# Gates of the grouped experts on GpSimd, and their last product in three passes on split values

## The chip, the cores and the metric

One core of one Trainium2 chip runs the whole program. The metric is the device time of one execution in microseconds (us), the median of the runs shown. TensorE is PE in the profile, VectorE is DVE, ScalarE is ACT, GpSimd is POOL and SyncE, which issues the DMAs here, is SP; PEld is PE's load of stationary weights.

## The reference, cut to what matters

The program is a tower of four layers on 64 x 32 = 2048 tokens of 128 channels: a choice of tokens, then four times an attention-like and an expert stage. The change lies in the first expert stage alone. It has 64 experts of 64 hidden channels; a router gives each token 8 of them with weights:

```
h  = silu(x @ w1[e]) * (x @ w3[e])
yb = h @ w2[e]
y  = sum over the 8 chosen e of  w[e] * yb
```

An expert takes at most 256 tokens. The kernel computes every expert for every token and multiplies by a gate that is zero where the token is not the expert's, so the expert stage does the same work for any routing.

## The kernel before, in words

The stage `grouped_experts` (line 721) works on 32 units of two experts: the hidden channels of both fill the 128 partitions. A unit has four steps, one for each group of 512 tokens, so there are 128 steps. The channels lie on the partitions and the tokens along the free axis.

A step goes like this. PE makes `pa` = x times w1 and `pb` = x times w3 in PSUM. Each is a `product` (line 303) of three passes in the format fp32r: the high part of the weights times the high part of x, the low part of the weights times the high part of x, and the high part of the weights times the low part of x. ACT makes the silu `S` of `pa` (line 815). DVE multiplies it by `pb` into `T2` ("bend", line 829), and by the gates `GS` into `HF` ("gate", line 838). PE multiplies `HF` by w2 and adds into one of four accumulators `acc` that stay in PSUM over all units (line 794): one product of plain fp32, which the trace records as two.

PE's order is written out by hand: step s of `pa` and `pb`, then the last product of step s - 2. `pa` and `pb` have two PSUM buffers each; a step waits until "bend" of the step before the last has read them (`t_ready`).

Weights come from `Weights` (line 311): SP loads a unit's 128 x 384 numbers (w1, w3, w2) into one of four buffers `W`, and POOL splits the first 256 columns into the high part (line 332, an addition of zero that rounds) and the low part (line 336, a subtraction). The first four units are split in the routing stage (`route_grouped`), where `start_splits` does it; the others are split by POOL as soon as their load has landed, and POOL does nothing else in the stage.

The gates: routing leaves a row of gates for each expert in DRAM; SP loads the two rows of a unit, each broadcast to 64 partitions (line 766), into one of three buffers `GS`. SP's queue is in program order: it waits for the buffer of unit u - 3, loads the gates of unit u, waits until the last products of unit u - 1 are done (`summed`), and loads the weights of unit u + 3.

Other stages do similar things. `quick_experts` (stage m3x) has its gates on POOL (line 634) with the weight splits between them, and its last product in fp32. `relu_experts` (stage m1x) splits its hidden values on chip: high part by ACT (line 500) or DVE, low part by DVE (line 532), then a product of three passes.

Of the kernel before, what the change touches and what calls it, by code (L numbers as in the profile page):

```python
# [13 lines left out]
F32 = mybir.dt.float32  # L14
BF16 = mybir.dt.bfloat16
F32R = mybir.dt.float32r
U32 = mybir.dt.uint32
ALU = mybir.AluOpType
ACT = mybir.ActivationFunctionType
AX = mybir.AxisListType  # L20

P = 128
# [4 lines left out]
GROUP = 512  # L27
GROUPS = T // GROUP
# [274 lines left out]
def product(pe, out, lhsT, rhs, start=True, stop=True):  # L303


    pe.matmul(out, lhsT[0], rhs[0], start=start, stop=False, skip_group_check=True)  # L306
    pe.matmul(out, lhsT[1], rhs[0], start=False, stop=False, skip_group_check=True)  # L307
    return pe.matmul(out, lhsT[0], rhs[1], start=False, stop=stop, skip_group_check=True)  # L308
# [43 lines left out]
class ReluWeights:  # L352


    RAW = 4
# [212 lines left out]
def quick_experts(nc, name, H, XR, ident, gateF, gate_rows, stored, weights, b2):  # L568


    UNITS = 16
    STEPS = UNITS * GROUPS
    RAW = weights.buffers
    W, WR, BX = weights.W, weights.WR, weights.BX
    w_loaded, w_split, bias_ready = weights.loaded, weights.split_made, weights.bias_ready
    with Stage(nc, name) as st:
# [28 lines left out]
        with nc.Block() as block:  # L605
            @block.sync
            def _(sp):
                sp.dma_start(B2[:, :], b2[:, :]).then_inc(bias_loaded, 16)
                sp.wait_ge(stored, 16 * GROUPS)
                for u in range(UNITS):  # L610
                    e = u // 2
                    if u % 2 == 0:
                        if e >= 2:
                            sp.wait_ge(gated, 2 * GROUPS * (e - 1))
                        sp.dma_start(GS[:, e % 2, :], gate_rows[e, :].partition_broadcast(P)).then_inc(g_loaded[e % 2], 16)
                    if u >= 1 and u + RAW - 1 < UNITS:
                        sp.wait_ge(summed, GROUPS * u)
# [103 lines left out]
def grouped_experts(nc, name, H, XR, ident, gate_rows, stored, weights):  # L721

    UNITS = 32
    STEPS = UNITS * GROUPS
    RAW = weights.buffers
    GB = 3  # L730
    W, WR = weights.W, weights.WR
    w_loaded, w_split = weights.loaded, weights.split_made
    with Stage(nc, name) as st:
        GS = st.sb("GS", [P, GB, T])
        S = st.sb("S", [P, 2, GROUP])
        T2 = st.sb("T2", [P, 2, GROUP])
        HF = st.sb("HF", [P, 3, GROUP])
        OT = st.sb("OT", [P, T])
        acc = [st.ps(f"acc{g}", [P, GROUP]) for g in range(GROUPS)]
        pa = [st.ps(f"pa{i}", [P, GROUP]) for i in range(2)]  # L740
        pb = [st.ps(f"pb{i}", [P, GROUP]) for i in range(2)]
        g_loaded = [st.sem(f"g_loaded{i}") for i in range(GB)]
        a_ready = st.sem("a_ready")
        b_ready = st.sem("b_ready")
        s_ready = st.sem("s_ready")
        t_ready = st.sem("t_ready")
        gated = st.sem("gated")
        summed = st.sem("summed")
        ot_ready = st.sem("ot_ready")
        turned = st.sem("turned")  # L750

        def place(s):
            return s // GROUPS, s % GROUPS

        def tokens(g):
            return slice(g * GROUP, (g + 1) * GROUP)

        with nc.Block() as block:
            @block.sync
            def _(sp):  # L760
                sp.wait_ge(stored, 16 * GROUPS)
                for u in range(UNITS):
                    if u >= GB:
                        sp.wait_ge(gated, GROUPS * (u - GB + 1))
                    for e in range(2):
                        sp.dma_start(GS[64 * e:64 * (e + 1), u % GB, :],
                                     gate_rows[2 * u + e, :].partition_broadcast(64)).then_inc(g_loaded[u % GB], 16)
                    if u >= 1 and u + RAW - 1 < UNITS:
                        sp.wait_ge(summed, GROUPS * u)
                        weights.load(sp, u + RAW - 1, (u + RAW - 1) % RAW)  # L770

            @block.gpsimd
            def _(pool):
                for u in range(RAW, UNITS):
                    pool.wait_ge(w_loaded[u % RAW], 16 * (u // RAW + 1))
                    weights.split(nc.gpsimd, u % RAW, u, None)

            @block.tensor
            def _(pe):
                def first(s):  # L780
                    u, g = place(s)
                    j = u % RAW
                    if g == 0:
                        pe.wait_ge(w_split, RAW + u + 1)
                    if s >= 2:
                        pe.wait_ge(t_ready, s - 1)
                    x = [XR[:, n, tokens(g)] for n in range(2)]
                    product(pe, pa[s % 2][:, :], [WR[:, j, n, 0:P] for n in range(2)], x).then_inc(a_ready, 1)
                    product(pe, pb[s % 2][:, :], [WR[:, j, n, P:2 * P] for n in range(2)], x).then_inc(b_ready, 1)

                def second(s):
                    u, g = place(s)
                    pe.wait_ge(gated, s + 1)
                    pe.matmul(acc[g][:, :], W[:, u % RAW, 2 * P:3 * P], HF[:, s % 3, :], start=(u == 0),  # L794
                              stop=(u == UNITS - 1), skip_group_check=True).then_inc(summed, 1)

                for s in range(STEPS + 2):
                    if s < STEPS:
                        first(s)
                    if s >= 2:  # L800
                        second(s - 2)
                for g in range(GROUPS):
                    pe.wait_ge(ot_ready, g + 1)
                    out = (pa[0], pa[1], pb[0], pb[1])[g]
                    for t in range(GT):
                        mm = pe.transpose(out[:, t * P:(t + 1) * P], OT[:, (g * GT + t) * P:(g * GT + t + 1) * P], ident[:, :])
                    mm.then_inc(turned, 1)

            @block.scalar
            def _(act):  # L810
                for s in range(STEPS):
                    act.wait_ge(a_ready, s + 1)
                    if s >= 2:
                        act.wait_ge(t_ready, s - 1)
                    nc.scalar.activation(S[:, s % 2, :], pa[s % 2][:, :], ACT.Silu).then_inc(s_ready, 1)  # L815
                for g in range(GROUPS):
                    act.wait_ge(summed, STEPS - GROUPS + g + 1)
                    nc.scalar.activation(OT[:, tokens(g)], acc[g][:, :], ACT.Copy).then_inc(ot_ready, 1)

            @block.vector  # L820
            def _(dve):
                v = nc.vector

                def bend(s):
                    dve.wait_ge(s_ready, s + 1)
                    dve.wait_ge(b_ready, s + 1)
                    if s >= 2:
                        dve.wait_ge(gated, s - 1)
                    v.tensor_tensor(T2[:, s % 2, :], S[:, s % 2, :], pb[s % 2][:, :], ALU.mult).then_inc(t_ready, 1)  # L829

                def gate(s):
                    u, g = place(s)
                    dve.wait_ge(t_ready, s + 1)
                    if g == 0:
                        dve.wait_ge(g_loaded[u % GB], 32 * (u // GB + 1))
                    if s >= 3:
                        dve.wait_ge(summed, s - 2)
                    v.tensor_tensor(HF[:, s % 3, :], T2[:, s % 2, :], GS[:, u % GB, tokens(g)], ALU.mult).then_inc(gated, 1)  # L838

                for s in range(STEPS + 1):  # L840
                    if s < STEPS:
                        bend(s)
                    if s:
                        gate(s - 1)
                for g in range(GROUPS):
                    t = slice(g * GT, (g + 1) * GT)
                    dve.wait_ge(turned, g + 1)
                    out = (pa[0], pa[1], pb[0], pb[1])[g]
                    v.tensor_tensor(H[:, t, :], H[:, t, :], out[:, :].rearrange("p (t c) -> p t c", c=P), ALU.add)
# [1961 lines left out]
def build(nc, ins, out):  # L2811
    Stage.spent = []
    with Stage(nc, "g") as st:
# [32 lines left out]
        with Stage(nc, "m0s") as s:  # L2846
            XR = s.sb("XR", [P, 2, T], F32R)
            GT_rows = s.sb("GT_rows", [64, T])
            gate_rows = nc.dram_tensor("m0_gate_rows", (64, T), F32, kind="Internal").ap()
            stored = s.sem("stored")  # L2850
            weights = Weights(nc, s, ins["L0_units"], 4, 2 * P, 0)
            route_grouped(nc, "m0r", XT, XR, ident, iota, consts["earlier"], ins["L0_ffn_gate_w"], ins["L0_ffn_gate_b"],
                          GT_rows, gate_rows, stored, weights)
            grouped_experts(nc, "m0x", H, XR, ident, gate_rows, stored, weights)
# [18 lines left out]
        with Stage(nc, "m3s") as s:  # L2873
# [4 lines left out]
            weights = Weights(nc, s, ins["L3_units"], 4, 2 * P, 3)  # L2878
# [108 lines left out]
```

## Time and profile before

| | us |
|---|---|
| runs of the kernel | 3297.12, 3297.83, 3304.19 (median 3297.83) |
| the profiled execution | 3300.3, with a span of 3298.5 from its first to its last instruction |
| the stage of the grouped experts in that span | 1295.0 to about 1592 |
| mean granted clock of PE over the span | 0.888 of full speed |

The profile is of one execution. A line of a timeline gives the start in us from the start of the span, the duration in us, the engine, the line of the kernel, the operation, what it writes and reads with partitions x elements, how many records are merged, and in brackets the idle time before it and what ended it. Names carry the stage: `m0x_` is the stage of the change, `m0s_` its weights.

### The profile page before, as it was taken

Reading aid. Unit: us, or ns where it says so; the run is one execution under the profiler, and the core shown is the slowest. Engines: PE = TensorE matmul, PEld = TensorE weight load, DVE = VectorE, ACT = ScalarE, POOL = GpSimd, SP = SyncE. Lnnn points to the kernel's source line nnn. Section 1 sums busy time; section 2 is a strip of 40 time slices with the busy share of each in tenths; the row PEclk is TensorE's granted clock in tenths of the full one; section 3 lists DMA queues with packets and bytes.
Section 4 is the critical chain, followed back from the end, with each engine's and each line's share of the span. In section 5 each row is a group of like instructions: output and inputs, shape, how many; then the busy total and the mean of one; then the engine's idle time right before and its main releaser. Section 6 shows DMA issues by size and latency. Waiting matters only on the chain. (4 is left out here: it accounts for less than half of the span.)

```text
span 3298.5 us, 29241 instructions
## 1 busy us (share of the span) xinstructions
PE 2573.4 (78%) x8955; PEld 1522.9 (46%) x8955; DVE 2360.9 (72%) x3401; ACT 1333.6 (40%) x2106; POOL 1386.7 (42%) x841
## 2 busy tenths in 40 slices
PE   1887877687787754999578978399997589768499
PEld 0333333332332322666346646377775467523365
DVE  5699798669979975555566575578886668669556
ACT  2644544264454421222243433167774257410222
POOL 1499699449969951111114334100001210024266
PEclk9899899889989886999789989599998789879799
DMA  4244155125505502556100000121210021000021
GB/s 135 41 122 109 20 130 108 29 41 122 109 20 129 109 21 56 138 137 150 33 17 10 16 0 4 36 76 60 76 57 13 3 89 52 17 13 13 11 81 64
DMA packets 86601, 203.32 MB, mean 62 GB/s; under 512 B 12816, under 2 KB 25184, under 8 KB 77920
## 3 DMA queue, kind: packets, MB, share of 16 engines
q1 hardware_dynamic: 85952, 200.63, 24.0%
q8 instruction: 63, 1.03, 0.1%
q0 software_dynamic: 512, 1.05, 0.1%
q14 instruction: 74, 0.61, 0.1%
HBM read 198.76 MB, written 2.88 MB: 61 GB/s over the span
## 5 line engine op out<-in xcount | busy, mean ns | idle before, releaser
L532 DVE TENSOR_TENSOR m1x_HS<-m1x_R,m1x_HS 128x512 fp32r<-128x512 f32 x256 | 175.8, 691 | 69.2 <-ACT m1x_HS L500 64.8
L493 ACT ACTIVATE m1x_R<-m1x_ph,m1s_W 128x512 f32<-128x512 f32 x256 | 176.3, 689 | 107.1 <-PE m1x_ph L308 106.3
L1337 POOL TENSOR_TENSOR t2x_KM<-t2x_KT,t2x_HM 128x2048 f32<-128x2048 f32 x8 | 28.8, 3603 | 434.8 <-ACT t2x_KT L1410 416.6
L1677 POOL TENSOR_TENSOR t3xs_QH<-t3xs_HS,t3xa_Q 128x1536 f32<-128x1536 f32 x16 | 62.0, 3877 | 352.6 <-DVE t3xs_HS L1663 352.6
L829 DVE TENSOR_TENSOR m0x_T<-m0x_S,m0x_pb 128x512 f32<-128x512 f32 x128 | 88.1, 689 | 128.3 <-PE m0x_pb L308 120.8
L2080 PE MATMUL t0x1fs_acc<-t0x1fs_HC,g_ident 128*128 128x512 f32 x256 | 134.1, 656 | 38.2 <-POOL t0x1fs_HC L2161 38.1
L2080 PE MATMUL t0x0fs_acc<-t0x0fs_HC,g_ident 128*128 128x512 f32 x256 | 135.0, 660 | 36.4 <-POOL t0x0fs_HC L2161 36.3
L815 ACT ACTIVATE m0x_S<-m0x_pa 128x512 f32<-128x512 f32 x128 | 76.6, 598 | 213.1 <-PE m0x_pa L308 213.1
L2080 PE MATMUL t0x1bs_acc<-t0x1bs_HC,g_ident 128*128 128x512 f32 x256 | 130.8, 641 | 37.1 <-POOL t0x1bs_HC L2161 37.0
L2080 PE MATMUL t0x0bs_acc<-t0x0bs_HC,g_ident 128*128 128x512 f32 x256 | 130.4, 640 | 35.8 <-POOL t0x0bs_HC L2161 35.7
L2161 POOL TENSOR_TENSOR t0x1bs_HC<-t0x1bs_HS,t0x1bs_CB 128x1024 f32<-128x1024 f32 x64 | 149.2, 2360 | 13.2 <-PE t0x1bs_acc L2080 6.6
L2161 POOL TENSOR_TENSOR t0x0bs_HC<-t0x0bs_HS,t0x0bs_CB 128x1024 f32<-128x1024 f32 x64 | 149.3, 2370 | 9.8 <-DMA t0x0bs_CB<-t0x0b_bc_rows 3.6
L2161 POOL TENSOR_TENSOR t0x1fs_HC<-t0x1fs_HS,t0x1fs_CB 128x1024 f32<-128x1024 f32 x64 | 149.1, 2370 | 6.0 <-DMA t0x1fs_CB<-t0x1f_bc_rows 4.5
L2161 POOL TENSOR_TENSOR t0x0fs_HC<-t0x0fs_HS,t0x0fs_CB 128x1024 f32<-128x1024 f32 x64 | 148.7, 2354 | 5.6 <-DMA t0x0fs_CB<-t0x0f_bc_rows 3.9
L332 POOL TENSOR_TENSOR m0s_WR<-m0s_W,m0s_ZERO 128x256 fp32r<-128x256 f32 x32 | 26.2, 820 | 260.7 <-DMA m0s_W<-in_L_units 260.5
L794 PE MATMUL m0x_acc<-m0x_HF,m0s_W 128*128 128x512 f32 x256 | 131.6, 596 | 5.3 <-DVE m0x_HF L838 5.3
L532 DVE TENSOR_TENSOR m2x_HS<-m2x_R,m2x_HS 128x512 fp32r<-128x512 f32 x128 | 87.9, 692 | 43.1 <-ACT m2x_HS L500 40.9
L493 ACT ACTIVATE m2x_R<-m2x_ph,m2s_W 128x512 f32<-128x512 f32 x128 | 88.2, 689 | 53.7 <-PE m2x_ph L308 53.3
L634 POOL TENSOR_TENSOR m3x_HF<-m3x_T,m3x_GS 128x512 f32<-128x512 f32 x64 | 81.6, 1280 | 59.1 <-DVE m3x_T L706 57.2
L306 PE MATMUL m1x_py<-m1x_HS,m1s_WR 128*128 128x512 f32 x256 | 103.3, 404 | 1.4 <-DVE m1x_HS L532 1.3
L306 PE MATMUL m0x_pa<-m0s_XR,m0s_WR 128*128 128x512 f32 x128 | 100.9, 788 | 1.8 <-PEq L890 1.8
L307 PE MATMUL m1x_ph<-m1s_XR,m1s_WR 128*128 128x512 f32 x256 | 102.3, 400 | 0.0
(908 smaller groups left out, 7652.2 us busy)
## 6 DMA issues: line engine op xcount, KB each, us to landing
m0x_GS<-m_gate_rows SPq DMA_DIRECT2D x64, 512.0 KB, 6.6
t0x0fs_CB<-t0x0f_bc_rows SPq DMA_DIRECT2D x32, 512.0 KB, 6.1
t0x0bs_CB<-t0x0b_bc_rows SPq DMA_DIRECT2D x32, 512.0 KB, 6.4
t0x1fs_CB<-t0x1f_bc_rows SPq DMA_DIRECT2D x32, 512.0 KB, 6.3
t0x1bs_CB<-t0x1b_bc_rows SPq DMA_DIRECT2D x32, 512.0 KB, 6.8
m1x_GS<-m_gate_rows SPq DMA_DIRECT2D x16, 1024.0 KB, 4.7
m1s_W<-in_L_w SPq DMA_DIRECT2D x16, 514.0 KB, 3.3
m2x_GS<-m_gate_rows SPq DMA_DIRECT2D x8, 1024.0 KB, 4.7
```

Of the source, the lines that this page charges most:

```text
L306: pe.matmul(out, lhsT[0], rhs[0], start=start, stop=False, skip_group_check=True)
L307: pe.matmul(out, lhsT[1], rhs[0], start=False, stop=False, skip_group_check=True)
L493: a.activation(R[:, s % 4, :], ph[s % 4][:, :], ACT.Relu, bias=W[:, e % RAW, weights.cut + c:weights.cut + c + 1]).then_inc(relu_ready, 1)
L532: v.tensor_tensor(HS[:, s % 4, 1, :], R[:, s % 4, :], HS[:, s % 4, 0, :].bitcast(F32), ALU.subtract).then_inc(low_made, 1)
L634: nc.gpsimd.tensor_tensor(HF[:, s % 3, :], T2[:, s % 2, :], GS[:, u // 2 % 2, tokens(g)], ALU.mult).then_inc(gated, 1)
L794: pe.matmul(acc[g][:, :], W[:, u % RAW, 2 * P:3 * P], HF[:, s % 3, :], start=(u == 0), stop=(u == UNITS - 1), skip_group_check=True).then_ ...
L815: nc.scalar.activation(S[:, s % 2, :], pa[s % 2][:, :], ACT.Silu).then_inc(s_ready, 1)
L829: v.tensor_tensor(T2[:, s % 2, :], S[:, s % 2, :], pb[s % 2][:, :], ALU.mult).then_inc(t_ready, 1)
L1337: nc.gpsimd.tensor_tensor(KM[:, i % 2, :, :], keys, spread(HM[:, :], W), ALU.mult).then_inc(km_made, 1)
L1677: nc.gpsimd.tensor_tensor(QH[:, j % 2, 0:SPLIT], HS[:, j % 2, 0:SPLIT], Q[:, 0:SPLIT], ALU.mult).then_inc(qh_pool, 1)
L2080: mm = pe.matmul(acc[:, dh, :], ident[:, :], HC[:, m % 3, dh, :], start=False, stop=False, skip_group_check=True)
L2161: nc.gpsimd.tensor_tensor(HC[:, m % 3, :, :], HS[:, m % 5, :, :], rows, ALU.mult).then_inc(hc_made, 1)
```

## The change

The gates move from DVE to POOL and to an earlier place: POOL multiplies the silu `S` by the gates into `SG`, and "bend" multiplies `SG` by `pb` into `HF`. ACT then copies `HF`, rounded, into the high half of `HR`, and DVE subtracts to get the low half ("low"). The last product takes three passes on the two halves of `HR` and of w2, so the weights are split in all 384 columns. It follows three steps behind instead of two (`LAG`). POOL's queue now holds the gates of every step, and the weight split of unit u + 1 behind the gates of step 1 of unit u. ACT's queue holds the silu of step s and then the copy of step s - 2. SP loads the gates of two units ahead, and of three units at the start. `first` waits for the silu ahead of `pa`, and for "bend" ahead of `pb`.

```diff
-    W, WR = weights.W, weights.WR
+    WR = weights.WR
+    LAG = 3
...
-        T2 = st.sb("T2", [P, 2, GROUP])
-        HF = st.sb("HF", [P, 3, GROUP])
+        SG = st.sb("SG", [P, 2, GROUP])
+        HF = st.sb("HF", [P, 2, GROUP])
+        HR = st.sb("HR", [P, 4, 2, GROUP], F32R)
...
-                for u in range(UNITS):
-                    if u >= GB:
-                        sp.wait_ge(gated, GROUPS * (u - GB + 1))
+
+                def load_gates(u):
                     for e in range(2):
                         sp.dma_start(GS[64 * e:64 * (e + 1), u % GB, :],
                                      gate_rows[2 * u + e, :].partition_broadcast(64)).then_inc(g_loaded[u % GB], 16)
+
+                for u in range(GB - 1):
+                    load_gates(u)
+                for u in range(UNITS):
+                    if u + GB - 1 < UNITS:
+                        if u:
+                            sp.wait_ge(gated, GROUPS * u)
+                        load_gates(u + GB - 1)
                     if u >= 1 and u + RAW - 1 < UNITS:
                         sp.wait_ge(summed, GROUPS * u)
                         weights.load(sp, u + RAW - 1, (u + RAW - 1) % RAW)
...
-                for u in range(RAW, UNITS):
-                    pool.wait_ge(w_loaded[u % RAW], 16 * (u // RAW + 1))
-                    weights.split(nc.gpsimd, u % RAW, u, None)
+                for s in range(STEPS):
+                    u, g = place(s)
+                    if g == 0:
+                        pool.wait_ge(g_loaded[u % GB], 32 * (u // GB + 1))
+                    pool.wait_ge(s_ready, s + 1)
+                    if s >= 2:
+                        pool.wait_ge(hidden, s - 1)
+                    nc.gpsimd.tensor_tensor(SG[:, s % 2, :], S[:, s % 2, :], GS[:, u % GB, tokens(g)], ALU.mult).then_inc(gated, 1)
+                    if g == 1 and RAW <= u + 1 < UNITS:
+                        pool.wait_ge(w_loaded[(u + 1) % RAW], 16 * ((u + 1) // RAW + 1))
+                        weights.split(nc.gpsimd, (u + 1) % RAW, u + 1, None)
...
                     if s >= 2:
-                        pe.wait_ge(t_ready, s - 1)
+                        pe.wait_ge(s_ready, s - 1)
                     x = [XR[:, n, tokens(g)] for n in range(2)]
                     product(pe, pa[s % 2][:, :], [WR[:, j, n, 0:P] for n in range(2)], x).then_inc(a_ready, 1)
+                    if s >= 2:
+                        pe.wait_ge(hidden, s - 1)
                     product(pe, pb[s % 2][:, :], [WR[:, j, n, P:2 * P] for n in range(2)], x).then_inc(b_ready, 1)

                 def second(s):
                     u, g = place(s)
-                    pe.wait_ge(gated, s + 1)
-                    pe.matmul(acc[g][:, :], W[:, u % RAW, 2 * P:3 * P], HF[:, s % 3, :], start=(u == 0),
-                              stop=(u == UNITS - 1), skip_group_check=True).then_inc(summed, 1)
-
-                for s in range(STEPS + 2):
+                    pe.wait_ge(low_ready, s + 1)
+                    product(pe, acc[g][:, :], [WR[:, u % RAW, n, 2 * P:3 * P] for n in range(2)],
+                            [HR[:, s % 4, n, :] for n in range(2)], u == 0, u == UNITS - 1).then_inc(summed, 1)
+
+                for s in range(STEPS + LAG):
                     if s < STEPS:
                         first(s)
-                    if s >= 2:
-                        second(s - 2)
+                    if s >= LAG:
+                        second(s - LAG)
...
-                for s in range(STEPS):
-                    act.wait_ge(a_ready, s + 1)
+                for s in range(STEPS + 2):
+                    if s < STEPS:
+                        act.wait_ge(a_ready, s + 1)
+                        if s >= 2:
+                            act.wait_ge(gated, s - 1)
+                        nc.scalar.activation(S[:, s % 2, :], pa[s % 2][:, :], ACT.Silu).then_inc(s_ready, 1)
                     if s >= 2:
-                        act.wait_ge(t_ready, s - 1)
-                    nc.scalar.activation(S[:, s % 2, :], pa[s % 2][:, :], ACT.Silu).then_inc(s_ready, 1)
+                        n = s - 2
+                        act.wait_ge(hidden, n + 1)
+                        if n >= 4:
+                            act.wait_ge(summed, n - 3)
+                        nc.scalar.activation(HR[:, n % 4, 0, :], HF[:, n % 2, :], ACT.Copy).then_inc(high_ready, 1)
...
                 def bend(s):
-                    dve.wait_ge(s_ready, s + 1)
+                    dve.wait_ge(gated, s + 1)
                     dve.wait_ge(b_ready, s + 1)
                     if s >= 2:
-                        dve.wait_ge(gated, s - 1)
-                    v.tensor_tensor(T2[:, s % 2, :], S[:, s % 2, :], pb[s % 2][:, :], ALU.mult).then_inc(t_ready, 1)
-
-                def gate(s):
-                    u, g = place(s)
-                    dve.wait_ge(t_ready, s + 1)
-                    if g == 0:
-                        dve.wait_ge(g_loaded[u % GB], 32 * (u // GB + 1))
-                    if s >= 3:
-                        dve.wait_ge(summed, s - 2)
-                    v.tensor_tensor(HF[:, s % 3, :], T2[:, s % 2, :], GS[:, u % GB, tokens(g)], ALU.mult).then_inc(gated, 1)
+                        dve.wait_ge(low_ready, s - 1)
+                    v.tensor_tensor(HF[:, s % 2, :], SG[:, s % 2, :], pb[s % 2][:, :], ALU.mult).then_inc(hidden, 1)
+
+                def low(s):
+                    dve.wait_ge(high_ready, s + 1)
+                    v.tensor_tensor(HR[:, s % 4, 1, :], HF[:, s % 2, :], HR[:, s % 4, 0, :].bitcast(F32),
+                                    ALU.subtract).then_inc(low_ready, 1)

                 for s in range(STEPS + 1):
                     if s < STEPS:
                         bend(s)
                     if s:
-                        gate(s - 1)
+                        low(s - 1)
...
-            weights = Weights(nc, s, ins["L0_units"], 4, 2 * P, 0)
+            weights = Weights(nc, s, ins["L0_units"], 4, 3 * P, 0)
```

## Rows read from the trace of the kernel before

**Rows 1.** The page, part 1: busy time, share and instructions of each engine.
```profile
PE 2573.4 (78%) x8955; PEld 1522.9 (46%) x8955; DVE 2360.9 (72%) x3401; ACT 1333.6 (40%) x2106; POOL 1386.7 (42%) x841
```

**Rows 2.** Windows: stretch, length, busy us of each engine, clock, DMA, GB/s.
```profile
1304.00:1310.00 6.00, 5.92 (x16) 3.78 (x17) 2.61 (x5) 0.91 (x2) 0.00 (x0) 0.73 0.45 94
...
1370.00:1390.00 20.00, 20.00 (x73) 13.39 (x72) 11.45 (x19) 5.38 (x9) 4.44 (x6) 1.00 0.64 152
...
3000.00:3040.00 40.00, 34.04 (x78) 14.15 (x77) 37.48 (x30) 0.00 (x0) 19.37 (x5) 1.00 0.06 16
```

**Rows 3.** Timeline of one step in the middle of the stage, PE and ACT.
```profile
1400.98 0.39 PE L307 MATMUL m0x_pa<-m0s_XR,m0s_WR 128*128 128x512 f32 x1
...
1401.21 0.40 PE L308 MATMUL m0x_pa<-m0s_XR,m0s_WR 128*128 128x512 f32 x1
...
1401.64 0.60 ACT L815 ACTIVATE m0x_S<-m0x_pa 128x512 f32<-128x512 f32 x1 [1.64 <-PE m0x_pa L308]
...
1403.22 0.39 PE L307 MATMUL m0x_pa<-m0s_XR,m0s_WR 128*128 128x512 f32 x1
```

**Rows 4.** Groups of instructions by line: busy us, mean ns, idle before.
```profile
L634 POOL TENSOR_TENSOR m3x_HF<-m3x_T,m3x_GS 128x512 f32<-128x512 f32 x64 | 81.6, 1280 | 59.1 <-DVE m3x_T L706 57.2 <-PE m3x_acc L657 1.1 <-issue 0.8
...
L336 POOL TENSOR_TENSOR m0s_WR<-m0s_W,m0s_WR 128x256 fp32r<-128x256 f32 x32 | 23.2, 726 | 2.5
...
L500 ACT ACTIVATE m1x_HS<-m1x_R 128x512 fp32r<-128x512 f32 x128 | 79.7, 623 | 0.0
...
L532 DVE TENSOR_TENSOR m1x_HS<-m1x_R,m1x_HS 128x512 fp32r<-128x512 f32 x256 | 175.8, 691 | 69.2 <-ACT m1x_HS L500 64.8
```

**Rows 5.** Timeline, DVE and POOL where they overlap, in two stages.
```profile
1214.69 4.50 POOL L1059 TENSOR_TENSOR g_H<-g_H,t0x1o_GB 128x2048 f32<-128x2048 f32 x1 [11.22 <-SPq L1027]
...
1217.96 1.27 DVE L91 TENSOR_TENSOR t0x1l_mean<-t0x1l_stats 128x16 f32<-128x16 f32 x1
1219.15 0.17 DVE L92 TENSOR_TENSOR t0x1l_gap<-t0x1l_stats 128x16 f32<-128x16 f32 x1
...
1315.52 0.68 DVE L838 TENSOR_TENSOR m0x_HF<-m0x_T,m0x_GS 128x512 f32<-128x512 f32 x1
1315.91 0.90 POOL L332 TENSOR_TENSOR m0s_WR<-m0s_W,m0s_ZERO 128x256 fp32r<-128x256 f32 x1 [62.71 <-DMA m0s_W<-in_L_units]
1316.89 0.72 POOL L336 TENSOR_TENSOR m0s_WR<-m0s_W,m0s_WR 128x256 fp32r<-128x256 f32 x1
1317.17 0.69 DVE L829 TENSOR_TENSOR m0x_T<-m0x_S,m0x_pb 128x512 f32<-128x512 f32 x1 [0.96 <-PE m0x_pb L308]
```

**Rows 6.** Timeline, gates on POOL in the stage m3x.
```profile
3149.65 0.75 DVE L706 SCALAR_TENSOR_TENSOR m3x_T<-m3x_pb,m3s_BX,m3x_T 128x512 f32<-128x512 f32 x1
...
3150.48 1.27 POOL L634 TENSOR_TENSOR m3x_HF<-m3x_T,m3x_GS 128x512 f32<-128x512 f32 x1 [0.53 <-DVE m3x_T L706]
...
3171.78 2.53 POOL L634 TENSOR_TENSOR m3x_HF<-m3x_T,m3x_GS 128x512 f32<-128x512 f32 x2
```

**Rows 7.** Timeline, the last early weight split, and the start and end of the stage.
```profile
1252.48 0.72 POOL L336 TENSOR_TENSOR m0s_WR<-m0s_W,m0s_WR 128x256 fp32r<-128x256 f32 x1
...
1303.34 0.69 DVE L838 TENSOR_TENSOR m0x_HF<-m0x_T,m0x_GS 128x512 f32<-128x512 f32 x1 [4.54 <-DMA m0x_GS<-m_gate_rows]
...
1304.09 2.07 PE L794 MATMUL m0x_acc<-m0x_HF,m0s_W 128*128 128x512 f32 x2 [4.69 <-DVE m0x_HF L838]
...
1306.81 0.60 PE L308 MATMUL m0x_pa<-m0s_XR,m0s_WR 128*128 128x512 f32 x1
1307.23 0.40 PE L306 MATMUL m0x_pb<-m0s_XR,m0s_WR 128*128 128x512 f32 x1
...
1309.03 0.40 PE L307 MATMUL m0x_pa<-m0s_XR,m0s_WR 128*128 128x512 f32 x1
...
1584.66 0.39 PE L307 MATMUL m0x_pa<-m0s_XR,m0s_WR 128*128 128x512 f32 x1
...
1589.44 0.60 ACT L818 ACTIVATE m0x_OT<-m0x_acc 128x512 f32<-128x512 f32 x1 [0.26 <-PE m0x_acc L794]
```

More of the change, by code:

```diff
@@ L745, in grouped_experts @@
         s_ready = st.sem("s_ready")
-        t_ready = st.sem("t_ready")
         gated = st.sem("gated")
+        hidden = st.sem("hidden")
+        high_ready = st.sem("high_ready")
+        low_ready = st.sem("low_ready")
         summed = st.sem("summed")
```

## The prediction

> **What bounds the kernel now.** The page's busy shares [rows 1] mix all stages and decide nothing here; only the stage of the grouped experts (1295 to 1592 us) changes. The windows [rows 2] show TensorE (PE) busy 20.00 of 20 us there at a granted clock of 1.00, the level of 2.4 GHz, with VectorE (DVE) at 11.45, ScalarE (ACT) at 5.38, GpSimd (POOL) at 4.44. So PE's own work is the bound. The timeline gives its step: from one second pass of the pa product (1400.98) to the next (1403.22) are 2.24 us [rows 3]. A split pass takes 0.23 us (1400.98 to 1401.21). Six make 1.38, so the plain fp32 product of line 794 takes 2.24 - 1.38 = 0.86. The stage is 32 units of 4 steps.
>
> **What the change takes off PE.** The fp32 product becomes three split passes, 3 x 0.23 = 0.69, and a step of nine passes 2.07 us: 0.17 us less, 21 us in 124 steps. The same three-pass product on values split on chip runs in stage m1x behind ACT's copy and DVE's subtraction [rows 4]. That is the gain, if PE stays the bound.
>
> **What it puts elsewhere.** Per step: the gates go from DVE (0.68, line 838 [rows 5]) to POOL, where the same 128x512 product takes 1.28 [rows 4], or 1.25 when it queues behind another (two in 2.53 [rows 6]); ACT gains a rounding copy, 0.62; DVE gains the subtraction ("low"), 0.69 [rows 4]. Per unit POOL also makes the weight split, now 384 columns wide, right behind the gates of step 1. No row has 384 columns; between 256 (0.73, line 336) and 512 (1.28) the middle is 1.00 each, ends 0.73 and 1.28. POOL's sum per unit is 4 x 1.28 + 2 x 1.00 = 7.1 of 8.28 us: by itself it fits. DVE, 1.38 of 2.07, and ACT, 1.22, fit too.
>
> **What doesn't fit: POOL and DVE don't read at once.** Rows 5 show it both ways. DVE's line 838 (both inputs in SBUF) ends at 1316.20; POOL's line 332, begun at 1315.91, ends 0.61 later and is 0.90 long. Line 336, begun later, beside no such instruction, takes 0.72. The other way round: line 91 of DVE, a 0.18 us instruction (line 92 takes 0.17), begins inside POOL's line 1059 and lasts 1.27, to 0.04 after POOL's end. So whichever comes second stands until the first is done, and then needs its duration less about 0.12 (0.72 - 0.61) of lead. Before, this meets one split half per unit, on an engine with 15 us to spare. "Low" reads HF and HR, both in SBUF; POOL's gates and splits read SBUF. "bend" reads PSUM for one input, as line 829 does, which at 1317.17 overlaps line 336 with no loss to either (0.69 and 0.72): I let it run free.
>
> Now one step, counted from its first PE pass. pa is done at 0.86 (its third pass starts at 0.46 and lasts 0.40); ACT's silu runs 0.89 to 1.49 [rows 3]; POOL starts 0.08 after its releaser ends (3150.40 to 3150.48 [rows 6]), the other hand-offs take 0.03 (silu after pa) to 0.08, which no term turns on: gates 1.57 to 2.85. ACT makes the copy for step s-2 right behind the silu, 1.51 to 2.13, so "low" of s-2 is always released inside the gates: it stands from 2.17 to 2.85 and ends 0.55 (0.69 less 0.14) later, at 3.40. "bend" of s follows, 3.44 to 4.13. The last product of s-2, queued behind pb of step s+1, is due at 2.07 + 1.38 = 3.45 and gets its data at 3.46. So a step without a weight split keeps 2.07 with nothing to spare.
>
> Step 1 of a unit, with the split, same zero. Gates end at 2.85; "low" takes its turn to 3.40; first half 3.40 + 0.88 = 4.28; "low" of step 0, behind bend, reads first again, to 4.93; second half 4.93 + 0.88 = 5.81. (Were the half first: 5.36, "low" to 5.91, gates of step 2 at 7.05: no difference.) Only now the gates of step 2, due at 3.64: to 7.06. bend 7.14 to 7.83. Queued behind it on PE is pb of the next unit's step 0, which needs bend's PSUM buffer: due 6.90, starts 7.88, ends 8.57. The gates of step 3 run to 8.31 and hold up "low" of step 1 to 8.86, so its last product, due at 8.57, runs 8.92 to 9.61. There the next unit's step 1 starts, with POOL idle and the same state as at the zero. A unit with a split takes 9.61 us, where the kernel before takes 4 x 2.24 = 8.96.
>
> PE's gaps, 0.98 and 0.35 us per unit, I cost without a fall of the clock: in the recurrence stage PE is busy 34.04 of 40 us at clock 1.00 [rows 2].
>
> How ready instructions take turns is not in the rows. My order (the one that stood first reads first) costs 1.33 us a unit over 8.28. Below: if no turn were lost, readings of 4 x 1.14 (gates behind a low), 4 x 0.55 and 2 x 1.00 make 8.76. Above: if a turn saves nothing of the second one's lead, the same walk gives 3.54 for "low", 4.54 and 6.23 for the halves ("low" between them to 5.23), 7.48 and 8.73 for the gates, 9.42 for "low" and 10.17 for the unit; a step without a split is then 2.22. I take 9.61, since line 332's row shows the lead saved (0.61 after the turn, not 0.72), and keep both ends.
>
> The Trainium skill, "SBUF — State Buffer", section "Who interferes with whom", has GpSimd and a VectorE instruction with two SBUF inputs exclude each other for the whole instruction, where rows 5 let about 0.12 overlap. By that letter every turn costs the full duration: an estimate of 10.17 a unit and some 3334 in all, against 3316.6 by rows 5.
>
> **Start, end, queues.** The first gates wait for their rows until 1303.34 [rows 7], as before: SP issues six loads instead of four, the first two at the head. Then 1.28 on POOL and 0.69 on DVE: pb of step 2 starts at 1305.45 (last product before: 1304.09). PE ran at the lower of its two levels for some 3.1 us after that wait (1304.09 to 1307.23 [rows 7]; mean clock of the window 0.73 [rows 2]). With as much again, seven passes of 0.42 (1306.81 to 1307.23), then five of 0.23 (rest of pb of step 3, first last product), step 4 starts at some 1309.7 to 1309.8; before it was 1308.8 (1309.03 less a pass): +1.0. At the end step 127 goes through gates, bend, copy, low and three passes: the last copy starts 6.45 after its first pass, against 1589.44 - 1584.43 = 5.01: +1.4. The first four weight splits, longer by 8 x 0.27 us on POOL, lie in the routing stage: the last ends at 1253.2 [rows 7], and nothing reads them before the stage starts at 1295: nothing, and 40 us of cover. Gates now load two units ahead; SP waits for the gates of u-1, some eight steps (16 us) before use: nothing either way.
>
> **Sum.** Steps 4 to 127 are 123. Before: 123 x 2.24 = 275.5. After: 28 units with a split, 28 x 9.61 = 269.1, and 11 steps of 2.07, 22.8: 291.9, so +16.4. With +1.0 and +1.4: +18.8 us on the span of 3298.5. The profiled execution took 3300.3; it would be 3319.1. The median of the runs shown, 3297.83, stands 2.5 below that execution, so I forecast 3316.6.
>
> **The rivals.**
> 1. PE stays the bound (faster). If "low" and POOL read side by side, low of step 1 is never held by gates and only the split's burst counts: gates of step 2 end at 1.57 + 1.28 + 2.08 + 1.25 = 6.18, bend 6.95, pb of the next step 0 waits from 6.90 to 7.0, some 0.1. A unit is then 8.4: 28 x 8.4 + 22.8 = 258.0, -17.5; with +1.0 and +1.0 (a shorter tail) -15.5: 3282. For it: lines 838 and 829 lose nothing before. Against: rows 5.
> 2. The turns pack (no change). At 8.76 per unit: 245.3 + 22.8 = 268.1, -7.4 + 2.4 = -5: 3293; at 9.0 to 9.1, +2 to +5. For it: two steps of a unit have POOL time over. Against: each later instruction is released by the one that stands, so idle turns occur.
> 3. Every turn costs more (slower still): 28 x 10.17 + 11 x 2.22 = 309.2, +33.7 + 2.4: 3334. For it: line 91 shows no lead saved, and POOL might win each tie and keep reading. Against: line 332.
>
> It decides at 8.96 us per unit: reading turns that add under 0.68 to 8.28 leave a gain.
>
> **How the numbers follow.** About 0.2% (6.6 us) is what a measurement can tell from no change. Chances: forecast 0.60, rival 3 0.07, both slower: 0.67; rival 2 0.13, same; rival 1 0.20, faster. The forecast's own range is 3306 to 3327. The range for 8 in 10 takes in rival 2, the nearer part of rival 1 (some 0.07 of its 0.20) and most of rival 3: 3284 to 3331.
>
> **What would show it.** Right: gates on POOL at 1.25 to 1.45 us each, "low" at 1.1 to 1.4 rather than 0.69 in most steps; a unit at 9.6 us; PE idle in the steady stage some 37 us in all, before pb's first pass with bend as releaser and before the last product with low as releaser. The three passes stand 0.23 apart. Wrong: "low" at 0.69 throughout and PE busy 20 of 20 us (rival 1), or a unit near 9.0 with few PE gaps (rival 2). PE's clock below 1.00 in the steady stage would break the sum on another side.

## The result and the profile after

The changed kernel takes 3311.55 us (median) against 3295.09 for the one before, measured on the same chip; the ratio is 1.0059, 95% interval [1.0044, 1.0073]: slower by 14 to 24 us. The forecast was 3316.6 and slower, +18.8 us.

The profiled execution after took 3308.08 us with a span of 3306.2, only 7.7 more than the span before. The stages that the change doesn't touch took some 11.5 us less in that execution, and executions of the kernel before alone spread over 22 us. So all readings below are made inside the stage: its **length** is counted from the first pass of pa to the start of the last copy of the accumulators (ACT's m0x_OT), its **unit** from the first pass of pa to that four steps later.

Before: 1295.01 to 1589.44 [rows 7], 294.4 us. After: 1291.69 to 1605.37, 313.7. That is **+19.3**, where the sum had +18.8.

The page of after, part 1, against [rows 1]:
```profile
PE 2562.3 (77%) x9083; PEld 1540.9 (47%) x9083; DVE 2413.2 (73%) x3401; ACT 1400.3 (42%) x2234; POOL 1598.6 (48%) x969
```
POOL gains 212 us for 128 more instructions, DVE 52 us for as many as before. The window in the middle of the stage, columns as in [rows 2]:
```profile
1370.00:1390.00 20.00, 18.66 (x77) 13.76 (x76) 13.31 (x16) 9.60 (x18) 17.30 (x14) 1.00 0.57 133
```
PE is no longer busy throughout (18.66 of 20), the clock is still 1.00, and POOL is at 17.30 where it was at 4.44. The groups by tile (ns min/median/max, first and last start) say what became long:
```profile
L793 POOL TENSOR_TENSOR m0x_SG<-m0x_S,m0x_GS x128: 1261/1290/1748, 1300.3 to 1600.3; 128x512 f32<-128x512 f32 x128
L858 DVE TENSOR_TENSOR m0x_HF<-m0x_SG,m0x_pb x128: 686/689/691, 1301.6 to 1602.2; 128x512 f32<-128x512 f32 x128
...
L862 DVE TENSOR_TENSOR m0x_HR<-m0x_HF,m0x_HR x128: 686/1137/1426, 1303.4 to 1603.6; 128x512 fp32r<-128x512 f32 x128
```
The bend (line 858, one input in PSUM) has one length; low (line 862, two inputs in SBUF) has any length from 0.69 to 1.43. One unit in the timeline after, matmuls reduced to first passes:
```profile
1402.65 0.39 PE L306 MATMUL m0x_pa<-m0s_XR,m0s_WR 128*128 128x512 f32 x1
...
1404.21 1.29 POOL L793 TENSOR_TENSOR m0x_SG<-m0x_S,m0x_GS 128x512 f32<-128x512 f32 x1 [1.26 <-ACT m0x_S L838]
1404.68 1.36 DVE L862 TENSOR_TENSOR m0x_HR<-m0x_HF,m0x_HR 128x512 fp32r<-128x512 f32 x1 [0.37 <-ACT m0x_HR L844]
1404.69 0.39 PE L306 MATMUL m0x_pa<-m0s_XR,m0s_WR 128*128 128x512 f32 x1
...
1405.46 1.47 POOL L332 TENSOR_TENSOR m0s_WR<-m0s_W,m0s_ZERO 128x384 fp32r<-128x384 f32 x1
...
1406.79 0.69 DVE L862 TENSOR_TENSOR m0x_HR<-m0x_HF,m0x_HR 128x512 fp32r<-128x512 f32 x1
1406.90 0.40 PE L306 MATMUL m0x_pa<-m0s_XR,m0s_WR 128*128 128x512 f32 x1
1407.00 1.35 POOL L336 TENSOR_TENSOR m0s_WR<-m0s_W,m0s_WR 128x384 fp32r<-128x384 f32 x1
...
1408.31 4.21 POOL L793 TENSOR_TENSOR m0x_SG<-m0x_S,m0x_GS 128x512 f32<-128x512 f32 x3
1408.95 0.39 PE L306 MATMUL m0x_pa<-m0s_XR,m0s_WR 128*128 128x512 f32 x1
1409.63 0.69 DVE L858 TENSOR_TENSOR m0x_HF<-m0x_SG,m0x_pb 128x512 f32<-128x512 f32 x1 [2.16 <-POOL m0x_SG L793]
...
1410.38 0.50 PE L306 MATMUL m0x_pb<-m0s_XR,m0s_WR 128*128 128x512 f32 x1 [0.58 <-DVE m0x_HF L858]
...
1411.43 0.50 PE L306 MATMUL m0x_acc<-m0x_HR,m0s_WR 128*128 128x512 f32 x1
...
1412.24 0.39 PE L306 MATMUL m0x_pa<-m0s_XR,m0s_WR 128*128 128x512 f32 x1
```
The reader can follow the walk of the prediction: gates to 1405.50, low stands beside them and ends 0.54 after (1406.04); the first half of the split begins meanwhile and ends 0.89 after low; low (0.69), the second half, and only then three gates in a row. The unit is 1412.24 - 1402.65 = 9.59.

### The profile page after: what moved, and what is told of

Read it like the earlier page. It is cut to its first block and busy times, and to the rows that moved or that the text cites. A ratio compares the mean times of both kernels' runs of the same rounds, so it can differ in the third digit from the quotient of the medians.

```text
span 3306.2 us, 29878 instructions
## 1 busy us (share of the span) xinstructions
PE 2562.3 (77%) x9083; PEld 1540.9 (47%) x9083; DVE 2413.2 (73%) x3401; ACT 1400.3 (42%) x2234; POOL 1598.6 (48%) x969
## 3 DMA queue, kind: packets, MB, share of 16 engines
q8 instruction: 64, 1.05, 0.1%
q0 software_dynamic: 512, 1.05, 0.1%
## 5 line engine op out<-in xcount | busy, mean ns | idle before, releaser
L793 POOL TENSOR_TENSOR m0x_SG<-m0x_S,m0x_GS 128x512 f32<-128x512 f32 x128 | 174.7, 1383 | 93.7 <-ACT m0x_S L838 46.8
L858 DVE TENSOR_TENSOR m0x_HF<-m0x_SG,m0x_pb 128x512 f32<-128x512 f32 x128 | 88.1, 688 | 89.4 <-POOL m0x_SG L793 76.3
L862 DVE TENSOR_TENSOR m0x_HR<-m0x_HF,m0x_HR 128x512 fp32r<-128x512 f32 x128 | 136.5, 1067 | 11.8 <-ACT m0x_HR L844 11.6
L307 PE MATMUL m1x_ph<-m1s_XR,m1s_WR 128*128 128x512 f32 x256 | 102.4, 400 | 0.0
L306 PE MATMUL m1x_ph<-m1s_XR,m1s_WR 128*128 128x512 f32 x256 | 102.4, 400 | 0.0
```

The costliest lines, as they stand in the source:

```text
L793: nc.gpsimd.tensor_tensor(SG[:, s % 2, :], S[:, s % 2, :], GS[:, u % GB, tokens(g)], ALU.mult).then_inc(gated, 1)
L858: v.tensor_tensor(HF[:, s % 2, :], SG[:, s % 2, :], pb[s % 2][:, :], ALU.mult).then_inc(hidden, 1)
L862: v.tensor_tensor(HR[:, s % 4, 1, :], HF[:, s % 2, :], HR[:, s % 4, 0, :].bitcast(F32), ALU.subtract).then_inc(low_ready, 1)
```

## The experiments

All lengths are read as above, each from one profiled execution. "Three-pass" is the last product on values split in high and low. The unit is one read near 1400 us; in the middle of the stage the others of a run lie within 0.06 us of it, except in e6, whose units go from 8.16 to 9.1, on average 8.32. Four runs with the same first steps (e2, e3, e4, e10) take 14.69 to 15.85 us from the stage's first pass to step 4, so a stage length is good to about 1 us.

| run | edit | unit us | stage us |
|---|---|---|---|
| before | | 8.96 | 294.4 |
| after | | 9.59 | 313.7 |
| e1 | low with one SBUF input | 8.47 | 282.3 |
| e2 | no weight splits | 8.58 | 286.6 |
| e3 | halves of the split apart | 8.98 | 296.6 |
| e5 | gates on POOL, last product plain | 8.96 | 297.5 |
| e7 | last product four steps behind | 9.22 | 302.4 |
| e6 | as e7, gates back on DVE | 8.16 (mean 8.32) | 273.9 |
| e8 | high and low made from PSUM | 9.04 | 297.0 |
| e4 | split on ACT and DVE | 10.38 | 337.7 |
| e10 | the same, a step earlier | 8.58 | 286.6 |
| e9 | as e7, high half a copy | 8.83 | 290.9 |
| e11 | as e6, high half a copy | 8.16 | 267.2 |

### Take one SBUF input from low (e1)
```diff
+held = st.ps("held", [P, GROUP])
...
-v.tensor_tensor(HR[:, s % 4, 1, :], HF[:, s % 2, :], HR[:, s % 4, 0, :].bitcast(F32),
+v.tensor_tensor(HR[:, s % 4, 1, :], held[:, :], HR[:, s % 4, 0, :].bitcast(F32),
```


> Leaves out: the subtraction 'low' reads a constant bank of PSUM in place of HF, and two groups of tokens share one accumulator, so that only the times mean something. Everything else is the changed kernel, whose unit with a weight split takes 9.59 us (PE's first pass of step 1 to that of the next unit) and whose stage takes 313.7 us (first PE pass to the last copy of the accumulators; 294.4 in the kernel before). Theory (a VectorE instruction with two inputs in SBUF and a GpSimd instruction take turns): 'low' now has one, falls from a median of 1.14 us to 0.69, GpSimd's weight split halves fall from about 1.4 to 1.0, a unit takes about 8.4 us, the stage about 313.7 - 28 x 1.2 = 280. Rival (the burst of weight split work on GpSimd is enough by itself, whoever reads): a unit stays near 9.6 and the stage near 313.

The groups by tile:
```profile
L866 DVE TENSOR_TENSOR m0x_HR<-m0x_held,m0x_HR x128: 682/691/693, 1306.8 to 1574.2; 128x512 fp32r<-128x512 f32 x128
```
Low has one length again, 0.69 in all 128, the halves take 1.02, the unit 8.47. In the steady units the same instructions run in the same order on the same engines; what differs is where one operand lies (and that two groups of tokens share an accumulator). So 1.12 of the 9.59 us of a unit are the turns. Rival 1 of the prediction (8.4) is what the change would have been without them. What is left over four undisturbed steps of 2.04 us, 0.3 us, comes where pb waits for the bend, as rival 1 has it of the split's burst. In the waits from 1310 to 1560 us (total us, times, longest) that is once a unit:
```profile
PEld m0x_pb L306 <- DVE m0x_HF L862: 11.3, 27, 0.4
```

### Take the split away, or pull its halves apart (e2, e3)
In e2 the lines of the split in POOL's loop are deleted. In e3:
```diff
+if g == 3 and RAW <= u + 2 < UNITS:
+    n, j = u + 2, (u + 2) % RAW
+    pool.wait_ge(w_loaded[j], 16 * (n // RAW + 1))
+    pool.tensor_tensor(WR[:, j, 0, :], weights.W[:, j, 0:weights.cut], weights.ZERO[:, :], ALU.add)...
...
 if g == 1 and RAW <= u + 1 < UNITS:
...
-    weights.split(nc.gpsimd, (u + 1) % RAW, u + 1, None)
...
+    pool.tensor_tensor(WR[:, j, 1, :], weights.W[:, j, 0:weights.cut], WR[:, j, 0, :]..., ALU.subtract)...
```


> Leaves out the weight splits inside the stage: units 4 to 31 use the split weights of units 0 to 3. Theory: 'low' still stands behind the gates in every step (1.1 to 1.4 us), but this costs PE nothing, since its product is due just when it ends: a step takes 2.07, a unit 8.3, the stage about 313.7 - 28 x 1.3 = 277. Rival (every turn between 'low' and the gates costs PE, the weight split only a part): a unit takes 8.8 to 9.2, the stage 291 to 303.

> Same work, only the two halves of a unit's weight split are apart: the first behind the gates of step 3 two units ahead, the second behind the gates of step 1 one unit ahead. Theory (turns, and a burst that is too long for the buffers to bridge): the walk of the prediction, done for this order, gives stalls of some 0.25 us at two places in a unit: 8.75 us, stage about 313.7 - 28 x 0.84 = 290. Rival (the sum of GpSimd's and VectorE's readings is what bounds a unit): the sum is the same, a unit stays near 9.6, the stage near 313.

Without splits the unit is 8.58: neither the 8.3 of the theory nor the 8.8 or more of the rival. The first passes of pa start at 1400.38, 1402.43, 1404.64, 1406.71 and 1408.96: two of four steps take 2.05 to 2.07, the other two 2.21 to 2.25, and the waits from 1310 to 1560 us show the last product's weights waiting for low 71 times:
```profile
PEld m0x_acc L306 <- DVE m0x_HR L859: 20.3, 71, 0.4
```
The gates' turn against low thus uses up all of the step's slack and a little more. The halves apart give 8.98: of the fall of 0.84 us that was expected 0.61 came, since each half still stands behind a low (1.47 each in the timeline); the four steps take 2.05, 2.56, 2.05 and 2.32.

### Each part of the change alone (e5, e7, e6)
e5 keeps the gates on POOL and leaves the last product plain (no copy, no low). e7 is the change with LAG = 4 and five buffers HR. e6 is e7 with the old order of gates on DVE:
```diff
-nc.gpsimd.tensor_tensor(SG[:, s % 2, :], S[:, s % 2, :], GS[:, u % GB, tokens(g)], ALU.mult)
...
-v.tensor_tensor(HF[:, s % 2, :], SG[:, s % 2, :], pb[s % 2][:, :], ALU.mult)
+v.tensor_tensor(T2[:, s % 2, :], S[:, s % 2, :], pb[s % 2][:, :], ALU.mult)
...
+v.tensor_tensor(HF[:, s % 3, :], T2[:, s % 2, :], GS[:, u % GB, tokens(g)], ALU.mult)
```


> The change without its last part: gates on GpSimd ahead of 'bend', gates loaded two units ahead, weight split in 256 columns in GpSimd's queue, but the last product in plain fp32 two steps behind, and so neither copy nor 'low'. No VectorE instruction of a step has two inputs in SBUF. Theory: PE is the bound again, 2.24 us per step, 8.96 per unit, the stage 294.4 plus 1 to 3 us for the later start: 295 to 298; GpSimd's gates take 1.28 and the split halves 0.73. Rival (the gates on GpSimd, with the weight split in their queue, delay the steps by themselves): a unit takes 9.3 or more, the stage 305 or more.

> The change with the last product one step later (four steps behind, five buffers of the halves), nothing else. Theory: the plain steps lose what they had too little (2.07 instead of up to 2.2), and of the two gaps of TensorE in a unit, 0.98 before the second projection and 0.35 before the last product, only the first stays: unit 9.1 to 9.3 us, stage 299 to 305 us. Rival (the round of GpSimd and VectorE itself is as long as the unit, and a longer lag buys nothing): unit 9.5 to 9.6, stage 311 to 314 us.

> The three-pass last product kept, the gates back on VectorE (as before), GpSimd only splits; last product four steps behind. VectorE then has three multiplies or subtractions of about 0.69 us in a step, 2.07, as long as TensorE's 2.07, and two of them read two SBUF inputs beside the split. Theory (turns): the split's halves of about 1.0 us hold one VectorE instruction each for 0.4 to 0.8 us, unit 8.8 to 9.4 us, stage 288 to 305 us, shorter than the change's 313.7 because a turn of VectorE is 0.69 and not 1.28. Rival (any three-pass form with a VectorE at its limit loses as much): unit 9.6 or more, stage 313 us or more. If VectorE slips past the split for nothing: unit 8.3, stage 278.

e5 and e7 came as their theories had it; e6's theory (288 to 305 us) missed, and its stage is shorter even than the third case it names (278). The windows from 1320 to 1550 us, columns as in [rows 2]; e7:
```profile
1320.00:1550.00 230.00, 212.52 (x910) 168.52 (x909) 169.07 (x201) 115.35 (x202) 202.37 (x149) 1.00 0.59 136
```
e6:
```profile
1320.00:1550.00 230.00, 228.57 (x998) 185.57 (x996) 229.85 (x330) 132.60 (x222) 79.20 (x56) 1.00 0.67 150
```
The four stages make a square. Gates on DVE: plain 294.4, three-pass 273.9 (e6), a gain of 20.5. Gates on POOL: plain 297.5 (e5), three-pass 302.4 (e7), a loss of 4.9. So the product alone, with its lag of four steps instead of two, gains 20.5 and the gates' move alone costs 3.1; together they are 25.4 us worse than the sum of the two (302.4 + 294.4 - 297.5 - 273.9). The start of the stage doesn't make this: between the pa products of steps 9 and 125 alone before, e6, e5 and e7 take 259.9, 241.0, 259.8 and 266.2 us, which gives 25.3. There the gates' move alone costs nothing; its 3.1 us come of a later start (step 4 at 17.2 us from the stage's first pass, against 13.8). What each lacks without the other is the pair that takes turns: gates on POOL at every step, and a low on DVE beside them. In e6 DVE is busy 229.85 of 230 us and PE still 228.57: a VectorE that is recorded as full costs little, as its instructions start 0.60 apart when they queue:
```profile
1399.72 0.67 DVE L850 TENSOR_TENSOR m0x_T<-m0x_S,m0x_pb 128x512 f32<-128x512 f32 x1
...
1400.32 0.68 DVE L859 TENSOR_TENSOR m0x_HF<-m0x_T,m0x_GS 128x512 f32<-128x512 f32 x1
...
1400.92 0.68 DVE L863 TENSOR_TENSOR m0x_HR<-m0x_HF,m0x_HR 128x512 fp32r<-128x512 f32 x1
...
1401.52 0.68 DVE L850 TENSOR_TENSOR m0x_T<-m0x_S,m0x_pb 128x512 f32<-128x512 f32 x1
```
Three make 1.80 of PE's 2.04, where I had written 2.07. The 0.24 left in each step take up most of the turns against the split, which are still there (28 lows of up to 1.51 us between 1320 and 1550 us) and lift the mean unit from 8.16 to 8.32. e6 takes 3272.73 us, ratio to before 0.9932 [0.9908, 0.9956]: faster.

### High and low from PSUM (e8)
```diff
-v.tensor_tensor(HF[:, s % 2, :], SG[:, s % 2, :], pb[s % 2][:, :], ALU.mult)
+v.tensor_tensor(pb[s % 3][:, :], SG[:, s % 2, :], pb[s % 3][:, :], ALU.mult)
...
-    n = s - 2
-    nc.scalar.activation(HR[:, n % 4, 0, :], HF[:, n % 2, :], ACT.Copy)
+    n = s - 1
+    nc.scalar.activation(HR[:, n % 4, 0, :], pb[n % 3][:, :], ACT.Copy)
...
-v.tensor_tensor(HR[:, s % 4, 1, :], HF[:, s % 2, :], HR[:, s % 4, 0, :].bitcast(F32),
+v.tensor_tensor(HR[:, s % 4, 1, :], pb[s % 3][:, :], HR[:, s % 4, 0, :].bitcast(F32),
```


> The change kept whole, but the product of gated silu and second projection is written back into its PSUM bank, so that the high half and the low half are made from PSUM and no VectorE instruction of the stage has two SBUF inputs (pa gets one buffer, pb three, the copy comes one step earlier). Theory (the turns of GpSimd and VectorE are the whole loss): low 0.68 to 0.72 us, gates 1.28 to 1.30, each half of the split about 1.02, unit 8.3 to 8.45 us, stage 277 to 283 us, 11 to 17 us faster than the kernel before. Rival (GpSimd's own work, 4 x 1.28 + 2 x 1.02 in a unit, or the PSUM bank held longer, sets the period): unit 8.9 us or more, stage over 294 us, no faster than before.

Every turn is gone (low 681/684/692 ns, gates 1261/1291/1301), and the unit is 9.04 all the same: 3296.82 us, ratio 1.0003 [0.999, 1.0016]. The rival holds, in its second half: GpSimd's own work is not what sets the period, since e1 has the same work in a unit of 8.47. The waits between 1310 and 1560 us:
```profile
ACT m0x_HR L843 <- DVE m0x_pb L855: 38.0, 50, 1.4
PEld m0x_pb L306 <- DVE m0x_HR L859: 24.8, 25, 1.0
POOL m0x_SG L792 <- DVE m0x_pb L855: 23.0, 31, 0.8
```
My edit put the copy one step earlier. It now stands on ACT waiting for the bend, with the next silu queued behind it; late silu makes late gates, and a late low holds the bank that pb needs. Each duration was right; by these waits the order on a third engine took the gain. No run moves the copy back, so this chain is read and not tested.

### The split on ACT and DVE (e4, e10)
```diff
-weights.split(nc.gpsimd, (u + 1) % RAW, u + 1, None)
...
+if g == 1 and RAW <= u + 1 < UNITS:
...
+    nc.scalar.activation(WR[:, j, 0, :], weights.W[:, j, 0:weights.cut], ACT.Copy)
...
+if g == 2 and RAW <= u + 1 < UNITS:
...
+    v.tensor_tensor(WR[:, j, 1, :], weights.W[:, j, 0:weights.cut], WR[:, j, 0, :].bitcast(F32), ALU.subtract)
```
e10 has g == 0 and g == 1 in these two places.

> GpSimd keeps only the gates; the high half of the weights is copied by ScalarE after its copy of step 1, the low half subtracted by VectorE in step 2. Theory (what is lost is the split's turns on GpSimd; VectorE's 0.69 + 1.35 of a step leaves it little room for the 0.6 us of the low half, but its wait for a turn shrinks when it comes later): unit 8.5 to 8.9 us, stage 284 to 295 us. Rival (the turns are paid wherever the split's two SBUF inputs are read): unit 9.3 us or more, stage over 304 us.

> The run with the weights' halves on ScalarE and VectorE once more, each half one step earlier, so that the low half is made about 2 us before the next unit's first product, which stood 1.55 us for it. Theory (that gap was my placement and not a turn): no wait of TensorE for the weights, unit 8.5 to 8.9 us, stage 282 to 295 us. Rival (VectorE has no room for the low half, 0.55 us in a unit beside 0.69 + 1.35 in each step): the wait moves to the last product or to the second projection and the unit stays at 9.3 us or more, stage over 304 us.

e4 missed by far: 3337.02 us, ratio 1.0135 [1.0109, 1.016]. Its timeline says why; the unit's first product waits for its weights:
```profile
1403.02 0.54 DVE L876 TENSOR_TENSOR m0s_WR<-m0s_W,m0s_WR 128x384 fp32r<-128x384 f32 x1
...
1403.62 0.50 PE L306 MATMUL m0x_pa<-m0s_XR,m0s_WR 128*128 128x512 f32 x1 [1.57 <-DVE m0s_WR L876]
```
DVE works so far behind PE that its "step 2" ends 1.5 us after the next unit's first product is due. A step earlier (e10) the wait is gone and the unit is 8.58, just that of e2, which has no splits. VectorE's 0.55 for the half costs nothing beside e2. Only that POOL does not make the split between its gates counts.

### A split half with one input, and the best of both (e9, e11)
```diff
-pool.tensor_tensor(WR[:, j, 0, :], weights.W[:, j, 0:weights.cut], weights.ZERO[:, :], ALU.add)
+nc.gpsimd.tensor_copy(WR[:, j, 0, :], weights.W[:, j, 0:weights.cut])
```


> The change with the last product four steps behind, and the high half of the weights made on GpSimd by a copy of one SBUF input instead of a sum of two (the weights and a tile of zeros). Theory (the turns are between instructions with two SBUF inputs on both engines): the copy shows one length in all units, at most 1.0 us, although a subtraction of VectorE starts beside it; then the low half of the weights starts about 0.5 us earlier, the gap of 0.8 us before the second projection shrinks by as much: unit 8.5 to 8.9 us, stage 280 to 292 us. Rival (any instruction of GpSimd on SBUF takes turns with VectorE's two-input ones, the number of its inputs decides nothing): the copy is lengthened to 1.3 us or more in the units where the sum took 1.47, unit 9.1 to 9.3 us, stage 299 to 305 us.

> The run with the gates on VectorE and the three-pass product, and the high half of the weights by a copy of one SBUF input: the two findings together. Theory (a copy on GpSimd takes no turn, so that VectorE loses only the turn against the low half, some 0.8 us in a unit, which its 0.27 us of room in each step wins back within the unit): copy 0.97 us, units of 8.16 to 8.25 us, stage 268 to 274 us, the shortest of all, 20 to 27 us under the kernel before. Rival (TensorE's passes and the waits of that run were the bound already): stage 273 to 276 us, no difference between the two.

e9's numbers came as the theory said (copy 968/969/976 ns, unit 8.83, stage 290.9), and **its reason fell** all the same. In e11 the copy takes 0.50 to 1.05. The timeline of e11, DVE and POOL:
```profile
1378.45 0.69 DVE L867 TENSOR_TENSOR m0x_HR<-m0x_HF,m0x_HR 128x512 fp32r<-128x512 f32 x1
1378.46 1.05 POOL L789 CAST m0s_WR<-m0s_W 128x384 fp32r<-128x384 f32 x1 [6.18 <-DMA m0s_W<-in_L_units]
...
1402.72 0.66 POOL L789 CAST m0s_WR<-m0s_W 128x384 fp32r<-128x384 f32 x1 [6.07 <-DMA m0s_W<-in_L_units]
1402.93 0.99 DVE L867 TENSOR_TENSOR m0x_HR<-m0x_HF,m0x_HR 128x512 fp32r<-128x512 f32 x1
...
1435.52 0.50 POOL L789 CAST m0s_WR<-m0s_W 128x384 fp32r<-128x384 f32 x1 [6.09 <-DMA m0s_W<-in_L_units]
1435.57 1.00 DVE L867 TENSOR_TENSOR m0x_HR<-m0x_HF,m0x_HR 128x512 fp32r<-128x512 f32 x1
```
Begun with low, the copy ends 0.37 after it (1379.51 and 1379.14); begun first, it makes low stand (ending 0.54 after the copy, 1403.92 and 1403.38). So a copy with one input takes turns like the sum of two; it is only half as long, 0.50 against 1.01. In e9 it always stood behind a low: 0.6 of waiting and 0.37 make its 0.97. My test could not tell the two apart, because I had not known the copy's own length; the rival's "the number of its inputs decides nothing" is what e11 shows. The Trainium skill, "SBUF — State Buffer", section "Who interferes with whom", has it so: a VectorE instruction with two SBUF inputs contends with any GpSimd instruction that reads SBUF.

With the copy holding low too, e11's own reason was half wrong: VectorE's turns in a unit are not one of 0.8 us but two of some 0.3 and 0.2 (low beside the copy 0.99, the gate beside the second half 0.91, where undisturbed they take 0.68). The stage came out below the expected 268 to 274.

e11 is the best version: 3265.72 us, ratio to before 0.9919 [0.9902, 0.9936], PE busy 230.00 of 230 us between 1320 and 1550, every step there 2.04. Against e6 the stage is 6.7 us shorter, 4.3 of it between steps 9 and 125; the intervals of the two ratios overlap, so that this difference is shown by the stage of one execution each.

## Why the prediction was right, point by point

- **The bound and the gain.** Nine passes were put at 2.07 a step; where nothing waits a step is 2.04 (e11), a pass 0.227. The gain of the three-pass product was put at 0.17 a step, 21 us in 124 steps; it is 2.24 - 2.04 = 0.20, some 25 us, where nothing waits. That e6's stage shows 20.5 is chance: its mean unit of 8.32 still has turns in it, and its start and end differ from those before.
- **The turns.** They decided, as forecast: e1 takes them away by the place of one operand and the unit falls from 9.59 to 8.47. Low was forecast at 1.1 to 1.4 in most steps: it is 1.1 or more in 70 of 128, and the four steps of a unit take 0.69, 1.14, 0.96 and 1.37. Gates were forecast at 1.25 to 1.45 each: those of step 0 take 1.74, a turn behind low that the walk left out. It costs nothing, as POOL then waits 1.26 for the next silu. The lead of some 0.12 us that a standing instruction saves was read from one row [rows 5], and held: low ends 0.54 after its turn in place of 0.69, the half 0.89 after (forecast 0.55 and 0.88). The prediction's rival 3 has line 91 against this, "shows no lead saved", and that reading is wrong: the row shows a lead of 0.14, as the instruction ends 0.04 after POOL's and is 0.18 long where it stands for nothing:
```profile
L91 DVE TENSOR_TENSOR m0n_mean<-m0n_stats x1: 185/185/185, 1233.3 to 1233.3; 128x16 f32<-128x16 f32 x1
```
- **The walk.** From the unit's zero at 1402.65: first half's end 4.28 (forecast 4.28), second half's 5.70 (5.81), pb of the next step 0 at 7.73 (7.88), last product 8.78 (8.92), unit 9.59 (9.61). The Trainium skill's rule, "SBUF — State Buffer", section "Who interferes with whom", by its letter gave an estimate of 10.17; the trace has 9.59, and 1.47 for the first half where the full 1.02 behind low would be 1.60.
- **Two sizes that cancelled.** The step "that keeps 2.07 with nothing to spare" was mis-sized. With passes at 0.227 the last product behind step 2's pb is due at 3.40 and starts at 3.45 (1406.10), 0.06 after low's end: a wait of 0.05, close to nothing as forecast, but the first pass after a stall costs 0.12 more (below), and that step takes 2.21. With this 0.12 in each, the three waits of a unit are 0.17 here (forecast nothing), 0.87 at pb (0.98) and 0.38 at the last product behind it (0.35). So 4 x 2.04 = 8.16 and waits of 1.43 make the unit, in place of 8.28 and 1.33: that the unit came within 0.02 is partly luck. e7, whose last product waits nowhere, has one gap of 1.05 at pb and a unit of 9.22.
- **PE idle.** Forecast "some 37 us" in the steady stage, by starts of passes: 1.43 x 28 = 40. By records it is less (15.4 us of 230 between 1320 and 1550 us), as a record of 0.39 lies over the start of the gap behind it.
- **Start and end.** Step 4 starts 14.86 us after the stage's first pass, 13.79 before: +1.07 (forecast +1.0). With the 14.69 to 15.85 of the four runs above, this closeness is luck: the forecast had the first gates start when they did before, and counted from the stage's first pass they start 0.28 later (8.61 against 8.33). The last copy starts 6.65 after the first pass of step 127 (1598.72), before 5.01: +1.6 (forecast +1.4). Steps 4 to 127 take 292.2 (forecast 291.9).
- **The queues and loads** cost nothing, as forecast: POOL waits for gates of a load once, before the first.
- **The clock** stayed at 1.00 in the steady stage with PE at 18.66 of 20, as the 34.04 of 40 in [rows 2] had it.

## What to carry to other kernels

Ask of every instruction moved to GpSimd what VectorE does at the same time with two inputs in SBUF, and lay both on one time line: sums per engine said that this change fits (7.1 of 8.28 us), the turns said that it doesn't. A part that pays can be hidden in a change that loses: the three-pass product alone is worth 20 us, the move of the gates, nearly free by itself, cost it. And when an instruction goes to another engine's queue, count how far that queue runs behind: e4 lost by order and not by duration, as e10 shows, and so did e8 as far as its waits tell.

## What the runs showed of the hardware that was not expected

- GpSimd's copy of 128x384 takes 0.50 us undisturbed (e11), its sum or difference of two such tiles 1.01 (e8).
- VectorE instructions of 0.68 us start 0.60 apart when they queue (e6); the sum of their durations overstates a full VectorE by an eighth.
- The first PE pass after a stall is recorded with 0.50 in place of 0.39, and its product takes 0.80 in place of 0.68 (e7: pb from 1404.33, the next product from 1405.13).
